# Eight linear-attention layers: centring by weights and TensorE, a split f32r feed-forward, and another order of the queues

## The reference, cut to what matters

```python
def _ln(x, g, b):
    m = mean(x); v = mean((x - m) ** 2)
    return (x - m) * rsqrt(v + 1e-05) * g + b
def layer(h, p):                      # 8 of them, 16 heads of 8
    q = elu(h @ wq + bq) + 1;  k = elu(h @ wk + bk) + 1;  v = h @ wv + bv
    kv = einsum('bshd,bshm->bhdm', k, v)
    z = 1.0 / (einsum('bshd,bhd->bsh', q, k.sum(axis=1)) + 1e-06)
    att = einsum('bshd,bhdm,bsh->bshm', q, kv, z)
    h = _ln(h + att @ wo + bo, g1, be1)
    y = gelu(h @ w1 + c1) @ w2 + c2   # 128 -> 512 -> 128, exact gelu
    return _ln(h + y, g2, be2)
x = x + _ln(layers(layernorm(x)), gf, bef)
```

## Time and profile before

| what | value |
| --- | --- |
| runs of the kernel before | 2200.87 us median of 3 (2197.51 to 2203.46) |
| the profiled execution: its own time | 2198.03 us |
| its span | 2196.3 us |
| busy in the span: PE, DVE, ACT, POOL | 1872.8, 1437.4, 1331.5, 534.0 us |
| mean granted TensorE clock, as a share of full speed | 0.942 |

### The profile page before, as it was taken

The page is one execution under the profiler, slowest core; times in us unless marked ns, Lnnn a source line. Parts: engine busy times, 40 slices in busy tenths (PEclk is TensorE's granted clock), DMA queues, the critical chain, the costliest instruction groups (busy, mean ns, idle before and its releaser), DMA issues.

```text
span 2196.3 us, 23770 instructions
## 1 busy us (share of the span) xinstructions
PE 1872.8 (85%) x8324; PEld 1055.0 (48%) x8324; DVE 1437.4 (65%) x2318; ACT 1331.5 (61%) x2118; POOL 534.0 (24%) x525
## 2 busy tenths in 40 slices
PE   8999999999999989997677778997577677777998
PEld 6886444344434437884233324783122223332786
DVE  6886564456445647886755554876998755652787
ACT  6997555555555558996365555555544545566554
POOL 1443000000000002444211122222699401113221
PEclk9999999999999999998888998998899769999899
DMA  3221000000000002220000000200000000000110
GB/s 97 82 68 54 1 17 17 0 17 17 17 0 17 10 10 74 68 73 29 1 1 1 1 1 1 83 25 0 10 4 30 1 0 1 1 1 1 51 57 19
DMA packets 23746, 52.39 MB, mean 24 GB/s; under 512 B 2336, under 2 KB 6816, under 8 KB 23648
## 3 DMA queue, kind: packets, MB, share of 16 engines
q1 hardware_dynamic: 23648, 51.12, 7.3%
HBM read 49.47 MB, written 1.64 MB: 23 GB/s over the span
## 4 chain that ended last, share of the span: by engine, by line
PE 56%; DVE 22%; ACT 15%; issue 4%; POOL 1%; DMA 1%; ACTq 0%; POOLq 0%; SPq 0%; DVEq 0%
PE ps L440 9%; PE ps L442 8%; PE ps L441 8%; PE ps L708 5%; DVE arena L1439 5%; DVE arena L1184 4%; PE ps L225 4%; PE ps L701 4%; PE ps L927 3%; ACT arena L1047 2%; PE ps L897 2%; ACT rstd L242 2%; ACT arena L997 2%; ACT rstd L238 2%; PE ps L886 2%
## 5 line engine op out<-in xcount | busy, mean ns | idle before, releaser
L548 DVE TENSOR_TENSOR hid_lo<-arena,hid_hi 128x512 fp32r<-128x512 f32 x384 | 342.7, 905 | 66.5 <-ACT arena L498 64.4
L1184 DVE TENSOR_REDUCE arena<-ps 128x1 f32<-128x512 f32 (+3 forms) x352 | 213.3, 639 | 87.3 <-PE ps L901 84.1
L526 POOL TENSOR_TENSOR w_lo<-wslot,w_hi 128x512 fp32r<-128x512 f32 x56 | 76.7, 1373 | 761.4 <-DVE w_hi L543 761.4
L1104 POOL TENSOR_SCALAR_AFFINE_SELECT arena<-arena 128x256 f32<-128x256 f32 x256 | 102.9, 408 | 459.7 <-ACT arena L1047 457.1
L440 PE MATMUL ps<-x_hi,w_hi 128*128 128x512 f32 x512 | 206.4, 403 | 0.3 <-DVE arena L630 0.3
L441 PE MATMUL ps<-x_lo,w_hi 128*128 128x512 f32 x512 | 204.0, 399 | 0.0
L442 PE MATMUL ps<-x_hi,w_lo 128*128 128x512 f32 x512 | 203.8, 398 | 0.0
L495 ACT ACTIVATE hid_hi<-ps,wslot 128x512 fp32r<-128x512 f32 x256 | 177.4, 693 | 32.2 <-PE ps L442 4.6
L1047 ACT ACTIVATE arena<-ps 128x1024 f32<-128x1024 f32 (+3 forms) x256 | 166.3, 705 | 47.6 <-PE ps L917 46.9
L897 PE MATMUL ps<-arena 128*128 128x512 bf16 (+3 forms) x512 | 134.4, 328 | 65.4 <-DVE arena L1184 36.4
L498 ACT ACTIVATE arena<-ps,wslot 128x512 f32<-128x512 f32 x256 | 175.1, 684 | 0.0
(11 more groups left out here) (223 smaller groups left out, 3857.1 us busy)
## 6 DMA issues: line engine op xcount, KB each, us to landing
arena<-gates_dram SPq DMA_DIRECT2D x96, 256.0 KB, 3.5
wslot<-pack_a SPq DMA_DIRECT2D x16, 514.5 KB, 3.6
wslot<-pack_b SPq DMA_DIRECT2D x8, 901.5 KB, 4.5
wslot<-pack_c SPq DMA_DIRECT2D x8, 768.0 KB, 4.4
res<-x_in SPq DMA_DIRECT2D x4, 256.0 KB, 5.0
out_dram<-res SPq DMA_DIRECT2D x4, 256.0 KB, 2.8
bc_dram<-arena SPq DMA_DIRECT2D x1, 384.0 KB, 3.2
arena<-bc_dram SPq DMA_DIRECT2D x16, 24.0 KB
```

Of the source, the lines that this page charges most:

```text
L548: dve.tensor_tensor(hid_lo[item % 2][:, k, :], hid32[:, k, :], hid_hi[item % 2][:, k, :].bitcast(F32), ALU.subtract).then_inc(S["hid_ok"], 1)
L1184: dve.tensor_reduce(neg_max[:, i, heads[0]:heads[-1] + 1:step], ps[:, bank, 0:len(heads) * keys].rearrange("p (m k) -> p m k", k=keys), AX ...
```

## The change

The weights of `Wo` and `W2` get their row mean subtracted on VectorE (`weights`, steps 0 and 1), so that the products come out centred. The residual is added in PSUM by two f32r matmuls with the matrix I - 1/128 (`centred`), so that both norms of a layer lose their mean matmul, their subtraction and the residual addition. `Wo` is folded into the masked key-value product: a transpose, a copy, a 128x128 matmul, a copy. The inverse denominators are packed to 128x256 and multiplied onto the queries instead of onto the attention. The variances of the middle norm are packed in one bank (`mid_var`), go once through `Ln` and `Exp` (`root`) and are spread by a matmul (`root_bc`). Queries and the feed-forward are split f32r products (`split3`); ScalarE writes the gelu twice for even blocks, VectorE rounds it for odd ones and makes every lo; GpSimd makes the lo parts of the layer input and of the weights. Keys and values of batch 0 are computed first, and the second norm of batches 0 to 2 is worked on while the feed-forward of the others runs, that of batch 3 at the head of the next layer. Loops are written out for the eight layers. The final norm takes the same form. The constants grow by 368 columns, the parameters by 16.

The diff, cut to its core; the lines are moved eight columns to the left. Unchanged lines begin with a space; SP loads layer l+2 into a slot once `out_high` of batch 3 of layer l is done, and stage A follows the same rule. In order: helpers and queue of TensorE, of ScalarE, of VectorE, then GpSimd and SP.

```diff
-CONSTS = [("ident", P), ("mean", P), ("block", P), ("head_sum", 32), ("head_spread", P),
+CONSTS = [("ident", P), ("mean", P), ("cent", P), ("block", P), ("head_sum", 16), ("spread_a", P), ("spread_b", P), ("pick", P),
...
-with pe.Fori(0, LAYERS // 2) as r:
...
+LN2_BANK = [3, 1, 2, 3]
+CUTS = [(B_WQ, B_WO), (B_W2, B_KVB)]
...
+    def split3(bank, w_at, s, hi, lo, lo_ready, stop, start=False):
+        w1, w2 = (t[s][:, w_at:w_at + P] for t in (wb_hi, w_lo))
+        pe.matmul(ps[:, bank, :], w1, hi, start=start, stop=False)
+        pe.matmul(ps[:, bank, :], w2, hi, start=False, stop=False)
+        lo_ready()
+        return pe.matmul(ps[:, bank, :], w1, lo, start=False, stop=stop)
+    def centred(bank, hi, lo, stop):
+        pe.matmul(ps[:, bank, :], cent_r[:, :], hi, start=True, stop=False)
+        return pe.matmul(ps[:, bank, :], cent_r[:, :], lo, start=False, stop=stop)
...
+    def last_var(l):
+        pe.wait_ge(S["blog_ok"], 4 * l + 1)
+        var(l, 3, LN2_BANK[3])
...
+        pe.wait_ge(S["w_parts"], c["parts"] + 2 * l + 2)
+        if l:
+            last_var(l - 1)
+        keys_values(0)
+        queries(0)
+        queries(1)
+        queries(2)
+        keys_values(1)
+        keys_values(2)
+        keys_values(3)
+        queries(3)
+        for b in range(NB):
+            pe.wait_ge(S["kf_ok"], m + b + 1)
+            pe.wait_ge(S["qf_ok"], m + b + 1)
...
+            pe.wait_ge(S["kvbd_ok"], m + b + 1)
+            pe.transpose(ps[:, b, 256:256 + P], kv_bd[:, b, :], ident).then_inc(S["kvt_mm"], 1)
+        for half in range(2):
             for b in range(NB):
+                mm = pe.matmul(ps[32 * b:32 * b + 32, 4, 0:256], ks_h[:, b, 16 - 16 * half:48 - 16 * half],
+                               qf[:, b, 256 * half:256 * half + 256], start=(half == 0), stop=(half == 1),
...
+            pe.wait_ge(S["kvt_ok"], m + b + 1)
+            pe.matmul(ps[:, b, 384:384 + P], kv_t[:, b, :], w[:, B_WO:B_WO + P], start=True,
+                      stop=True).then_inc(S["g_mm"], 1)
...
+        def residual(b):
+            pe.wait_ge(S["g_ok"], m + b + 1)
+            centred(b, h_hi[:, b, :], h_lo[:, b, :], False)
+        residual(0)
+        residual(1)
+        pe.wait_ge(S["rz_ok"], l + 1)
+        for b in range(NB):
+            for half, spread in enumerate(("spread_a", "spread_b")):
+                mm = pe.matmul(ps[:, 4 + b, 256 * half:256 * half + 256], ccol(spread)[32 * b:32 * b + 32],
+                               rz[32 * b:32 * b + 32, :], start=True, stop=True)
+            mm.then_inc(S["z_bc"], 1)
+        residual(2)
+        residual(3)
...
+        for b in range(NB):
+            pe.wait_ge(S["qz_ok"], m + b + 1)
+            pe.matmul(ps[:, b, :], kv_bd[:, b, :], qf[:, b, :], start=False,
+                      stop=True).then_inc(S["o_mm"], 1)
+            if b:
+                mid_var(b - 1)
+        mid_var(NB - 1)
+        pe.wait_ge(S["root_ok"], l + 1)
+        for b in range(NB):
+            pe.matmul(ps[:, 4 + b, :], ccol("pick")[32 * b:32 * b + 32], root[32 * b:32 * b + 32, :],
+                      start=True, stop=True).then_inc(S["root_bc"], 1)
...
+        def ff1(b, k):
+            n = FC * b + k
+            if k == 0:
+                pe.wait_ge(S["mid_hi_ok"], m + b + 1)
+            if n < 3:
+                pe.wait_ge(S["mid_xc"], m + n + 1)
+            else:
+                pe.wait_ge(S["gelu_ok"], 16 * l + n - 2)
+            split3(n % 3, B_W1 + k * P, s, mid_hi[:, b, :], mid_lo[:, b, :],
+                   lambda: pe.wait_ge(S["mid_lo_ok"], m + b + 1), True, True).then_inc(S["ff1_mm"], 1)
+        def ff2(b, k):
+            if k == 0:
+                centred(4 + b, mid_hi[:, b, :], mid_lo[:, b, :], False)
+            pe.wait_ge(S["gelu_lo"], 16 * l + FC * b + k + 1)
+            mm = split3(4 + b, B_W2 + k * P, s, hb_b[b % 2][:, k, :], lb_b[b % 2][:, k, :],
+                        lambda: None, k == FC - 1)
+            if k == FC - 1:
+                mm.then_inc(S["ff2_mm"], 1)
...
+        for item in range(NB + 1):
+            for k in range(FC):
+                if item < NB:
+                    ff1(item, k)
+                if item:
+                    ff2(item - 1, k)
+                if item == 2 and k == 1:
+                    pe.wait_ge(S["mid_xc"], m + 4)
+                    var(l, 0, LN2_BANK[0])
+                if item == NB and k < 2:
+                    pe.wait_ge(S["gelu_ok"], 16 * l + 14 + k)
+                    var(l, 1 + k, LN2_BANK[1 + k])
...
+    def root_of(l, b, bank):
+        act.wait_ge(S["bvar_mm"], 4 * l + b + 1)
+        act.activation(rstd[:, b, :], ps[:, bank, :], ACT.Ln, bias=eps).then_inc(S["blog_ok"], 1)
+        act.wait_ge(S["blog_ok"], 4 * l + b + 1)
+        act.activation(rstd[:, b, :], rstd[:, b, :], ACT.Exp, scale=-0.5).then_inc(S["brs_ok"], 1)
...
+        else:
+            root_of(l - 1, 3, LN2_BANK[3])
+        queries(0)
+        if l:
+            out_high(l - 1, 3, before)
+        keys(0)
+        queries(1)
+        queries(2)
+        keys(1)
+        keys(2)
+        keys(3)
+        queries(3)
+        for b in range(NB):
+            act.wait_ge(S["kvt_mm"], m + b + 1)
+            act.activation(kv_t[:, b, :], ps[:, b, 256:256 + P], ACT.Copy).then_inc(S["kvt_ok"], 1)
+        act.wait_ge(S["den_mm"], l + 1)
+        act.activation(rz, ps[:, 4, 0:256], ACT.Identity, bias=tiny).then_inc(S["den_ok"], 1)
...
+        for b in range(NB):
+            act.wait_ge(S["o_mm"], m + b + 1)
+            act.activation(sq[:, b, :], ps[:, b, :], ACT.Square, bias=c_bias[:, l:l + 1]).then_inc(S["mid_sq"], 1)
+        act.wait_ge(S["mid_var"], m + 4)
+        act.activation(root, ps[:, 4, :], ACT.Ln, bias=eps).then_inc(S["log_ok"], 1)
+        act.wait_ge(S["log_ok"], l + 1)
+        act.activation(root, root, ACT.Exp, scale=-0.5).then_inc(S["root_ok"], 1)
+        act.preload_act_table_set("gelu_and_others")
...
+        mid_high(0)
+        mid_high(1)
+        gelu(0, 0)
+        mid_high(2)
+        gelu(0, 1)
+        gelu(0, 2)
+        mid_high(3)
+        gelu(0, 3)
+        for b in range(1, NB):
+            for k in range(FC):
+                gelu(b, k)
+                if b >= 2 and k == 0:
+                    square(b - 2)
+        act.preload_act_table_set("natural_log_exp_and_others")
+        root_of(l, 0, LN2_BANK[0])
+        square(2)
+        root_of(l, 1, LN2_BANK[1])
+        out_high(l, 0, w)
+        root_of(l, 2, LN2_BANK[2])
+        out_high(l, 1, w)
+        square(3)
+        out_high(l, 2, w)
...
+    def weights(l, step):
+        s = l % 2
+        if step == 0:
+            dve.wait_ge(S[f"w_in{s}"], w_count(c, l))
+            square_w = wslot[:, s, B_WO:B_KVB].rearrange("p (a n) -> p a n", n=P)
+            dve.tensor_reduce(w_sum[:, :], square_w, AX_X, ALU.add).then_inc(S["w_sum_ok"], 1)
+        elif step == 1:
+            square_w = wslot[:, s, B_WO:B_KVB].rearrange("p (a n) -> p a n", n=P)
+            dve.wait_ge(S["w_sum_ok"], l + 1)
+            dve.scalar_tensor_tensor(out=square_w, in0=w_sum[:, :].unsqueeze(2).to_broadcast([P, 1 + FC, P]),
+                                     scalar=-1.0 / P, in1=square_w, op0=ALU.mult,
+                                     op1=ALU.add).then_inc(S["w_mid_ok"], 1)
+        else:
+            a, b = CUTS[step - 2]
+            dve.wait_ge(S["w_mid_ok"], l + 1)
+            dve.tensor_copy(wb_hi[s][:, a:b], wslot[:, s, a:b]).then_inc(S["w_hi_ok"], 1)
...
+    def scaled(l, b, bank, bias):
+        dve.wait_ge(S["brs_ok"], 4 * l + b + 1)
+        dve.scalar_tensor_tensor(out=rstd[:, b, :], in0=ps[:, bank, :], scalar=bias, in1=rstd[:, b, :],
+                                 op0=ALU.add, op1=ALU.mult).then_inc(S["by_ok"], 1)
+    def shifted(n, b, dst, g, be, done):
+        dve.wait_ge(S["by_ok"], n + b + 1)
+        dve.tensor_scalar(dst[:, b, :], rstd[:, b, :], g, be, ALU.mult, ALU.add).then_inc(done, 1)
...
+    for step in range(4):
+        weights(0, step)
...
+        keys_values(0)
+        if l:
+            scaled(l - 1, 3, 7, c_bias[:, LAYERS + l - 1:LAYERS + l])
+            shifted(2 * m - 4, 3, ha, before[:, B_G2:B_G2 + 1], before[:, B_BE2:B_BE2 + 1], S["h_ok"])
+        queries(0)
+        keys(0)
+        queries(1)
+        queries(2)
+        keys_values(1)
+        keys_values(2)
+        keys(1)
+        keys_values(3)
+        keys(2)
+        keys(3)
+        queries(3)
...
+        if l + 1 < LAYERS:
+            weights(l + 1, 0)
+        dve.wait_ge(S["den_ok"], l + 1)
+        dve.reciprocal(rz, rz).then_inc(S["rz_ok"], 1)
+        if l + 1 < LAYERS:
+            weights(l + 1, 1)
+        for b in range(NB):
+            dve.wait_ge(S["z_bc"], m + b + 1)
+            dve.tensor_tensor(qf[:, b, :], qf[:, b, :], ps[:, 4 + b, :], ALU.mult).then_inc(S["qz_ok"], 1)
...
+        for b in range(NB):
+            dve.wait_ge(S["mid_sq"], m + b + 1)
```

(86 more changed lines are left out.)

342 lines of the change are left out of this document (178 added, 164 removed).

## The result

Six runs of the changed kernel have a median of 2220.05 us (2215.79 to 2227.79), six of the kernel before 2202.03: a ratio of 1.0084, 95% interval [1.0062, 1.0106]. The change makes the program slower, by about 18 us; the forecast was 2183. The profiled execution took 2217.32 us (before 2198.03).

The account below looks back on a forecast made before the run. Taken to bound a layer: VectorE and ScalarE queues, then TensorE from the first `ff2`. Way in +11, seven periods of -3.25, way out -7, constants +0.7 give -18 on 2198.0: 2180 profiled, median 2183, range 2163 to 2208.

Parts of the forecast that it names:

- way in: Start of stage B: layer 0's weights prepared after the norm, first keys at 227, last gelu at 289; costs 11 us.
- seven periods: Layer to layer in stage B: each period 69.3 us against 72.56, a gain of 3.25 each.
- way out: Last gelu to the following stage's last subtraction: 26 us against 33.3, a gain of 7.
- TensorE's idle stretches: Waits at G+5.5 (2.0 us; G is a layer's last gelu), before keys 3 (2.6), around the root, before first `ff2` (2.0).
- Rival A: TensorE's clock falls in its waits, slowing keys 3 and the head of `ff1`: 3.2 us a layer, 2209; chance 0.15.
- To the first keys: From a layer's last gelu to keys of batch 0: 8.3 us, against 13.56 to the next products before.
- Queries and keys: G+8.3 to 25.9 (G is a layer's last gelu): a ping-pong of VectorE and ScalarE, nothing gained or lost.
- Middle: Mask to first `ff1`, G+25.9 to 43.55 (G is a layer's last gelu): 17.65 us against 18.73 before.
- Feed-forward: First `ff1` to last gelu: head bound by VectorE, 2.05 us a batch, then TensorE; 25.7 us against 22.6.
- The sum of TensorE's own work: TensorE's busy time in a layer falls from 67.6 to about 54 us.
- rival B: TensorE stays the bound to a larger part, other waits overrated: another 3 us less a layer, 2159; chance 0.12.
- rival D: ScalarE changes tables between gelus for Identity and Square: 8 x 1.28 us a layer, 2200 to 2220; chance 0.04.

Follow-up runs that it names:

- the fillers: Changed kernel plus 31 unread bf16 matmuls a layer in five of TensorE's waits: 2204.96 us, ratio 1.0003 against the kernel before.
- the best kernels: Changed kernel with both VectorE queue orders, layer 0's weights early and unread matmuls, 23 or 10 a layer: 2185.51 and 2185.59 us.
- two reorderings: VectorE's queue in the changed kernel: biases of keys 1, 2 before queries 1, 2 (2205.22 us); middle norm's next product before the lo (2206.66 us).
- the fuller form: Changed kernel with both VectorE queue orders, layer 0's weights early and 23 unread matmuls a layer: 2185.51 us, ratio 0.9906 against the kernel before.

## Why the prediction was wrong

The forecast said 2180 for the profiled execution, and it took 2217.3. By its own terms, the 37 us are: way in, last gelu of layer 0 at 291.6 instead of 289 + 0.7, 1.9; seven periods, 515.8 instead of 485.1, 30.7; way out, 28.4 instead of 26, 2.4; the unchanged code behind, 2.5.

**The step that failed is the price of zero for TensorE's idle stretches.** The forecast listed them correctly (2.0 and 2.6 us, the way around the root, and 2.0 before the first `ff2`; measured 1.98, 2.42, 1.44 with 1.68, and 1.76), but let them cost nothing beyond their own length. Rival A said what would follow, with a chance of 0.15. It is what happened: 16 of the 30.7 us. The rival's size was 3.2 a layer in all eight; it is 4.0 in four of seven periods, 2.3 on the mean, just the point from which it was said to decide. Its places were the keys 3 and the head of `ff1`; it left out the last variance with the first keys (0.9 of the 4.0), and in the short layers the head of `ff1` does run at the lower clock, at no cost. What spoke against it in the prediction, 0.96 in a window of stage D, did not carry over to this stage. Nor could a layer of before show it: the longest wait of TensorE in it is 0.76 us (its row below). That idle time and not load lowers the clock is shown by the fillers: with 31 matmuls more a layer the clock rises to 1.00 and the time falls.

```profile
461.76 3.70 PE L692 MATMUL ps<-arena,wslot 128*128 128x512 f32 x8 [0.76 <-DVE arena L792]
```

**The other half is the chain of the queues, 71.4 against 69.3 at the good clock.** In the short layer at 442.35 the marks are G+8.76, the last mask at 468.90 (G+26.55), first `ff1` G+44.92, first `ff2` 8.31 behind it, last gelu G+71.52. In the order of the forecast's sections:

- To the first keys +0.46. `out_high` is an Identity whose scale is a pointer, and occupies ScalarE for 0.70 from start to start (446.71 to 447.42, recorded with 0.80), where 0.60 was taken from gelus. The two that stand in the way are 0.2 of the 0.46; the rest was not looked into.
- Queries and keys +0.2. The ping-pong was read rightly; but what was taken as given, the order of VectorE's queue, was worth 1.3 (42.07 to 40.78).
- Middle +0.7. The chain of products and variances of the middle norm goes at 2.03 a batch, not 2 x 0.86 (the rows below). Why was not tested.
- Feed-forward 26.6 instead of 25.7. Its head was named as bound by VectorE, and is: 2.24 a batch, not 2.05, because `mid_high` takes 0.81 between two operations of VectorE. The order of the product and the lo is worth 1.0 (29.3 to 28.3).

```profile
475.25 1.88 PE L763 MATMUL ps<-arena 128*128 128x512 f32 x4
478.03 1.12 PE L763 MATMUL ps<-arena 128*128 128x512 f32 x2
480.06 1.12 PE L763 MATMUL ps<-arena 128*128 128x512 f32 x2
```
```profile
485.68 0.69 DVE L1041 TENSOR_TENSOR rstd<-rstd,ps 128x512 f32<-128x512 f32 x1 [2.98 <-PE ps L770]
486.41 0.55 DVE L966 TENSOR_SCALAR sq<-rstd,wslot 128x512 f32<-128x512 f32 x1
487.32 0.69 DVE L1031 TENSOR_TENSOR mid_lo<-sq,mid_hi 128x512 fp32r<-128x512 f32 x1 [0.37 <-ACT mid_hi L880]
487.93 0.68 DVE L1041 TENSOR_TENSOR rstd<-rstd,ps 128x512 f32<-128x512 f32 x1
```

The sum of TensorE's own work has a slip too: the terms listed come to 56.3 us a layer, not 54. Only rival B leans on it.

**What was right.** TensorE's busy time fell by 8 us in a short layer and the period by 1.2; the feed-forward got longer (26.6 against 22.6) though TensorE works less in it. The way in is longer by 13.8 us, and preparing layer 0's weights early gave back 8.2 of them. The way out is shorter (28.4 against 33.3), and the 16 denominators take 1.07 us, near the lower bound. No table is loaded between gelus: in each layer one load of ScalarE stands before the first and one behind the last, so rival D is out. Rival B, with TensorE as the bound, had no part. The 69.1 us of the best kernels lie near the forecast 69.3, but by luck: they need two reorderings that the forecast did not have, while the kernel it was made for takes 71.4 at the good clock.

**What stays open.** Why the clock falls four times in one layer and once in its neighbour, with the same waits. And in the fastest kernels the code behind stage B took 1390.0 (the fuller form) and 1386.1 us, where before had 1377.3. A stretch of 120 us, 280 behind the end of the stage, has a lower clock (before, then the fuller form):

```profile
1099.03:1219.03 120.00, 90.12 (x704) 38.51 (x704) 69.58 (x159) 69.95 (x117) 20.92 (x52) 0.87 0.00 1
```
```profile
1077.57:1197.57 120.00, 92.93 (x648) 37.96 (x650) 64.63 (x155) 66.53 (x115) 19.34 (x49) 0.79 0.00 1
```

The changed kernel has 0.85 there and loses 2.5 us in all behind the stage; that with the early weights, without a filler, has 0.83 and loses 9.3. So fillers are not needed for it, and the cause is not known; the runs of the kernel before alone scatter by 17 us (2195.96 to 2212.93). Of the 21.5 us gained in stage B (end at 797.57, before 819.03) the profiled execution of the fuller form shows only 8.7.

## What to carry to other kernels

A change that takes work off the engine that binds can open waits on it, as here. Where that engine is TensorE, price each wait twice, once as time and once as the lower clock for what follows (here 4.0 us in a layer of 71.4), and take a profile without waits as no evidence that the clock bears them. When TensorE's sum has fallen below the period, write the queues of the other engines out in time and look at which instruction stands in front of the one that TensorE waits for: two reorderings cost nothing and were worth more than the f32r feed-forward. If a short wait can't be removed, a few unread products in it can hold the clock, as 10 a layer did here in six of seven layers.
